# First-stage edge tiles of a graph layer handled in pairs, with the unread matmuls moved

## What is computed

```python
xm = x @ W_n2m;  e = edge_attr @ W_edge
q, k, v = xm @ W_q + b_q, xm @ W_k + b_k, xm @ W_v + b_v
alpha = sum(q[dst] * (k[src] + e @ W_e), per head) / 4
alpha = softmax of alpha over the edges of one dst
out = segment_sum((v[src] + e @ W_e) * alpha, dst)
x_r = xm @ W_skip + b_skip
beta = sigmoid([out, x_r, out - x_r] @ W_beta)
x = layernorm(x + (beta * x_r + (1 - beta) * out) @ W_m2n)
# second layer: x = layernorm(x + relu(x @ w1 + b + segment_sum(ew * (x @ w2)[src], dst)))
```

## Time and profile before

| what | value |
|---|---|
| median of three runs | 1742.92 us |
| span of the profiled execution, first to last instruction | 1705.3 us |
| that execution's time outside the span | not given by the profile |
| busy in the span: PE, DVE, ACT, POOL | 1245.0, 1346.5, 1225.0, 1042.2 us |
| unread matmuls of the first stage (L554) | 784, 118.5 us busy |
| granted TensorE clock, mean of the span | 0.926 of full |

### The profile page before, as it was taken

One profiled execution on the slowest core, in us unless ns is written; L12 is line 12 of the kernel. 1 busy time (PEld: TensorE's weight loads), 2 busy tenths in 40 slices (PEclk: granted clock), 3 DMA queues, 4 the chain that ended last, 5 costly groups with the idle time before them and its releaser, 6 DMA issues.

```text
span 1705.3 us, 34722 instructions
## 1 busy us (share of the span) xinstructions
PE 1245.0 (73%) x9184; PEld 1095.8 (64%) x9184; DVE 1346.5 (79%) x5156; ACT 1225.0 (72%) x4231; POOL 1042.2 (61%) x1182
## 2 busy tenths in 40 slices
PE   1888888888888882288877876788888876665661
PEld 1877777777777772177766766666666675554551
DVE  2777898889999998888877876799999984654653
ACT  0899999999999995077787876899999962222221
POOL 2666666555566660055555656888888846666665
PEclk9999999999999996599999997999999997787876
DMA  6899999999999996734444445899999942222221
GB/s 189 269 306 302 305 305 304 303 302 301 305 301 305 308 300 233 240 117 152 154 144 140 156 141 168 270 289 292 293 289 294 292 143 77 79 82 74 86 77 38
DMA packets 210148, 372.00 MB, mean 218 GB/s; under 512 B 36740, under 2 KB 67821, under 8 KB 208935
## 3 DMA queue, kind: packets, MB, share of 16 engines
q1 hardware_dynamic: 120822, 200.48, 37.2%
q10 hardware_dynamic: 57771, 108.12, 17.3%
q0 software_dynamic: 31360, 61.17, 13.2%
HBM read 231.39 MB, written 161.37 MB: 230 GB/s over the span
## 4 chain that ended last, share of the span: by engine, by line
ACT 36%; DVE 29%; issue 11%; another core or an unknown queue 9%; PE 9%; DMA 1%; POOL 1%; SPq 1%; DVEq 1%; ACTq 0%; POOLq 0%
ACT hout L728 10%; ACT scan_buf L728 10%; DVE stats L992 7%; DVE hpre L1238 6%; ACT big L756 4%; ACT em L688 3%; DVE big L1228 3%; DVE hpre L1314 2%; ACT lv L769 2%; PE pd L596 2%; DVE hout L1002 2%; DVE scan_buf L1002 2%; PE pd L597 2%; PE pk L619 2%
## 5 line engine op out<-in xcount | busy, mean ns | idle before, releaser
L992 DVE BATCH_NORM_STATS2 stats<-hpre 128x6 f32<-128x256 f32 x882 | 334.8, 421 | 1.8
L466 POOL DMA_INDIRECT ring_a<-in_x,gidx x196 | 185.6, 947 | 207.4 <-PE pt L556 146.7
L728 ACT ACTIVATE scan_buf<-hpre,nb,rs 128x128 f32<-128x128 f32 x686 | 292.1, 480 | 2.8 <-DVE scan_buf L1002 1.3
L728 ACT ACTIVATE hout<-hpre,nb,rs 128x128 f32<-128x128 f32 x686 | 292.2, 480 | 2.5 <-issue 1.2
L1098 DVE SCALAR_TENSOR_TENSOR hpre<-pd,beta,xg 128x128 f32<-128x128 f32 x784 | 221.3, 345 | 29.0 <-DVE beta L1091 1.0
L565 PE MATMUL pd<-w_sx,scan_buf 128*128 128x129 f32 x1568 | 229.7, 276 | 0.0
L469 POOL DMA_INDIRECT ring_b<-in_x,gidx x196 | 185.0, 944 | 60.0 <-issue 60.0
L619 PEld LDWEIGHTS pk<-w_sb,scan_buf 128*128 128x128 f32 x1568 | 211.5, 196 | 7.4
L499 POOL DMA_INDIRECT big<-h_tab,gidx x196 | 193.4, 987 | 35.0 <-POOL big L505 29.5
L619 PE MATMUL pk<-w_sb,scan_buf 128*128 128x128 f32 x1568 | 209.9, 278 | 0.0
L565 PEld LDWEIGHTS pd<-w_sx,scan_buf 128*128 128x128 f32 x1568 | 207.0, 192 | 2.7
(11 more groups left out here) (208 smaller groups left out, 3692.4 us busy)
## 6 DMA issues: line engine op xcount, KB each, us to landing
xg<-in_x SPq DMA_DIRECT2D x196, 256.0 KB
scan_buf<-in_xT SPq DMA_DIRECT2D x196, 256.0 KB
val<-h_tab SPq DMA_DIRECT2D x139, 256.0 KB
h_tab<-hout ACTq DMA_DIRECT2D x98, 256.0 KB
h_tab<-scan_buf ACTq DMA_DIRECT2D x98, 256.0 KB
out_z<-hout ACTq DMA_DIRECT2D x98, 256.0 KB
out_z<-scan_buf ACTq DMA_DIRECT2D x98, 256.0 KB
h_two<-h_tab SPq DMA_DIRECT2D x57, 256.0 KB, 9.1
```

The lines of the kernel that those rows point to most:

```text
L466: gp.indirect_dma_start(out=ring_a[:, u, :], out_offset=None, in_=x[:, :], in_offset=bass.IndirectOffsetOnAxis(ap=gidx[:, k, 0:1], axis=0))\
L728: ins = act.activation(hout[ju][:, i * D:(i + 1) * D], hpre[:, ju, i * D:(i + 1) * D], ACT.Identity, bias=nb_of(ju, i), scale=rs_of(ju, i))
L992: ins = dve.bn_stats(stats[:, ju, i, :, :].rearrange("p j s -> p (j s)"), two)
```

## The change

Tiles are worked on in pairs e = k // 2. The transposes of both tiles go to one bank of `pt`, in the order in which they stand in `xT_two`, and one copy of 512 columns moves them in odd steps. The products of both tiles are made in one odd step (k = 2e + 3), one tile in each bank of `pk`; v, q, the multiply and the sum of both follow in the next even step with one instruction each. `v_a`, `q_a`, `pr_a`, `al_a`, `xsT_a` and `kv_a` count pairs. Two unread matmuls (WARM) stand ahead of the products of each tile and write to the unused half of its `pk` bank; the four ahead of the transposes are gone. The softmax pieces start six steps behind instead of two (LAG_S), and four steps with such pieces alone are added at the end.

```diff
--- before.py
+++ after.py
@@ -25,6 +25,8 @@
 LEAD = 60.0
 NZ = 3
 NP = 1
+WARM = 2
+LAG_S = 6
 QSCALE = 1.0 / C ** 0.5
 
 
@@ -332,7 +334,7 @@
                 if j >= 0 and j % 2 == 0:
                     if j == 2 * E1:
                         sp.wait_ge(S["ea_cp2"], 16)
-                    wait(sp, S["kv_a"], j - 2)
+                    wait(sp, S["kv_a"], j // 2 - 1)
                     sp.dma_start(pair[0:R, j // 2 % 2, :], eaT_s[j // 2, :, :]).then_inc(ring["ea_in"][j // 2 % 2], 16)
                 if live(k, 0, T):
                     wait(sp, S["pre_d1"], k - U + 1)
@@ -532,28 +534,29 @@
             pe.wait_ge(S["id1"], 1)
 
             for k in range(T + 2):
-                if k > 1:
-                    j = k - 2
-                    pe.wait_ge(S["xsT_a"], j + 1)
-                    pe.wait_ge(ring["ea_in"][j // 2 % 2], 16 * (j // 4 + 1))
-                    if j > 1:
-                        pe.wait_ge(S["v_a"], j - 1)
-                        pe.wait_ge(S["pr_a"], j - 1)
-                    pe.matmul(pk[:, j % 2, 0:3 * DM], pair[:, j // 2 % 2, j % 2 * P:(j % 2 + 1) * P], b_kvq[:, :],
-                              start=True, stop=False)
-                    pe.matmul(pk[:, j % 2, 0:2 * DM], xT_two[:, j + 2, :], a_kv[:, :], start=False, stop=False)
-                    pe.matmul(pk[:, j % 2, 2 * DM:3 * DM], xT_two[:, j, :], a_q[:, :], start=False, stop=True)\
-                        .then_inc(S["kv_a"], 1)
+                if k > 2 and k % 2 == 1:
+                    e = (k - 3) // 2
+                    pe.wait_ge(S["xsT_a"], e + 1)
+                    pe.wait_ge(ring["ea_in"][e % 2], 16 * (e // 2 + 1))
+                    if e > 0:
+                        pe.wait_ge(S["v_a"], e)
+                        pe.wait_ge(S["pr_a"], e)
+                    for i in range(2):
+                        for w in range(WARM):
+                            pe.matmul(pk[:, i, 2 * P:4 * P], ones3[:, :], bias3[:, 0:2 * P], start=True, stop=True)
+                        pe.matmul(pk[:, i, 0:3 * DM], pair[:, e % 2, i * P:(i + 1) * P], b_kvq[:, :],
+                                  start=True, stop=False)
+                        pe.matmul(pk[:, i, 0:2 * DM], xT_two[:, 2 * e + 2 + i, :], a_kv[:, :], start=False, stop=False)
+                        mm = pe.matmul(pk[:, i, 2 * DM:3 * DM], xT_two[:, 2 * e + i, :], a_q[:, :], start=False, stop=True)
+                    mm.then_inc(S["kv_a"], 1)
                 if k < T:
-                    u = k % U
+                    u, e, i = k % U, k // 2, k % 2
                     pe.wait_ge(ring["xs_in"][u], 16 * (k // U + 1))
                     pe.wait_ge(ring["xd_in"][u], 16 * (k // U + 1))
-                    if k > 1:
-                        pe.wait_ge(S["xsT_a"], k - 1)
-                    for w in range(4):
-                        pe.matmul(pt[:, u % 2, 2 * P:4 * P], ones3[:, :], bias3[:, 0:2 * P], start=True, stop=True)
-                    pe.transpose(pt[:, u % 2, 0:P], ring_b[:, u, :], ident[:, :])
-                    pe.transpose(pt[:, u % 2, P:2 * P], ring_a[:, u, :], ident[:, :]).then_inc(S["t_a"], 1)
+                    if i == 0 and e > 1:
+                        pe.wait_ge(S["xsT_a"], e - 1)
+                    pe.transpose(pt[:, e % 2, i * P:(i + 1) * P], ring_b[:, u, :], ident[:, :])
+                    pe.transpose(pt[:, e % 2, (2 + i) * P:(3 + i) * P], ring_a[:, u, :], ident[:, :]).then_inc(S["t_a"], 1)
 
                     pe.wait_ge(ring["xgT_in"][u], 16 * (k // U + 1))
                     if k > 1:
@@ -739,22 +742,24 @@
 
             def step_a(k, u, it):
                 c = k // TC - 1
-                if 0 <= c < 3 and k % TC == 2 + 5:
+                if 0 <= c < 3 and k % TC == LAG_S + 5:
                     chunk_exps(c)
-                if live(k, 2, T):
-                    j, ju, _ = back(k, u, it, 2)
-                    wait(act, S["kv_a"], j + 1)
-                    wait(act, S["pr_a"], j - 1)
-                    kv = pk[:, ju % 2, DM:2 * DM].rearrange("p (h c) -> p h c", h=H)
-                    vo = val[:, :, :, j] if isinstance(j, int) else \
-                        val[:, :, :, bass.ds(j, 1)].rearrange("p h c a -> p h (c a)")
-                    act.activation(vo, kv, ACT.Copy).then_inc(S["v_a"], 1)
-                    act.activation(q_sb[:, ju % 2, :], pk[:, ju % 2, 2 * DM:3 * DM], ACT.Copy).then_inc(S["q_a"], 1)
+                if k % 2 == 0 and 0 <= k - 4 < T:
+                    e = (k - 4) // 2
+                    act.wait_ge(S["kv_a"], e + 1)
+                    if e > 0:
+                        act.wait_ge(S["pr_a"], e)
+                    kv = pk[:, :, DM:2 * DM].rearrange("p i (h c) -> p h c i", h=H)
+                    act.activation(val[:, :, :, 2 * e:2 * e + 2], kv, ACT.Copy).then_inc(S["v_a"], 1)
+                    act.activation(q_sb[:, :, :], pk[:, :, 2 * DM:3 * DM], ACT.Copy).then_inc(S["q_a"], 1)
+                if k % 2 == 1 and k < T:
+                    e = k // 2
+                    act.wait_ge(S["t_a"], 2 * e + 2)
+                    if e > 0:
+                        act.wait_ge(S["kv_a"], e)
+                    act.activation(xT_two[:, 2 * e:2 * e + 4, :], pt[:, e % 2, :].rearrange("p (a n) -> p a n", a=4),
+                                   ACT.Copy).then_inc(S["xsT_a"], 1)
                 if live(k, 0, T):
-                    wait(act, S["t_a"], k + 1)
-                    wait(act, S["kv_a"], k - 1)
-                    act.activation(xT_two[:, k:k + 3:2, :], pt[:, u % 2, 0:2 * P].rearrange("p (a n) -> p a n", a=2),
-                                   ACT.Copy).then_inc(S["xsT_a"], 1)
                     wait(act, S["mm_d1"], k + 1)
                     wait(act, S["pre_d1"], k - 1)
                     exp_minus(act, em[:, u % 2, :], pd[:, u % 2, :, D], -1.0, S["cl_d1"], S["em_d1"], k)
@@ -1045,11 +1050,11 @@
                                               row[:, a - 1:a] if c else 0.0, ALU.mult, ALU.add)
 
             def scan_piece(k):
-                c, s = (k - 2) // TC - 1, (k - 2) % TC
+                c, s = (k - LAG_S) // TC - 1, (k - LAG_S) % TC
                 if c < 0:
                     return
                 if s < 2:
-                    dve.wait_ge(S["al_a"], (c + 1) * TC)
+                    dve.wait_ge(S["al_a"], -(-(c + 1) * TC // 2))
                     last_piece()
                     local_max(c, 2 * s)
                     piece_done(local_max(c, 2 * s + 1))
@@ -1061,7 +1066,7 @@
                     cut_runs(c).then_inc(S["log_a"], 1)
                 elif 7 <= s < 15:
                     dve.wait_ge(S["sc_act"], c + 1)
-                    dve.wait_ge(S["v_a"], (c + 1) * TC)
+                    dve.wait_ge(S["v_a"], -(-(c + 1) * TC // 2))
                     weigh(c, 2 * (s - 7), 4)
                     piece_done(weigh(c, 2 * (s - 7) + 1, 4))
                 elif s >= 15:
@@ -1070,22 +1075,21 @@
                     piece_done(run_scan(c, 2 * (s - 15) + 1))
 
             def step_a(k, u, it):
-                if live(k, 2, T):
-
-                    j, ju, _ = back(k, u, it, 2)
-                    wait(dve, S["q_a"], j + 1)
-                    dve.scalar_tensor_tensor(out=prod[:, ju % 2, :], in0=pk[:, ju % 2, 0:DM], scalar=QSCALE,
-                                             in1=q_sb[:, ju % 2, :], op0=ALU.mult, op1=ALU.mult).then_inc(S["pr_a"], 1)
+                e = (k - 4) // 2
+                pairs = k % 2 == 0 and 0 <= e < T2
+                if pairs:
+                    dve.wait_ge(S["q_a"], e + 1)
+                    dve.scalar_tensor_tensor(out=prod[:, :, :], in0=pk[:, :, 0:DM], scalar=QSCALE, in1=q_sb[:, :, :],
+                                             op0=ALU.mult, op1=ALU.mult).then_inc(S["pr_a"], 1)
                 scan_piece(k)
                 if live(k, 0, T):
                     wait(dve, S["em_d1"], k + 1)
                     dve.tensor_scalar(ep[:, u % 2, :], em[:, u % 2, :], -1.0, -1.0, ALU.mult, ALU.add)\
                         .then_inc(S["ep_d1"], 1)
-                if live(k, 2, T):
-                    wait(dve, S["pr_a"], j + 1)
-                    ao = alpha[:, :, j:j + 1] if isinstance(j, int) else alpha[:, :, bass.ds(j, 1)]
-                    dve.reduce_sum(ao, prod[:, ju % 2, :].rearrange("p (h c) -> p h c", h=H), AX_X)\
-                        .then_inc(S["al_a"], 1)
+                if pairs:
+                    dve.wait_ge(S["pr_a"], e + 1)
+                    dve.reduce_sum(alpha[:, :, 2 * e:2 * e + 2].rearrange("p h i -> p i h"),
+                                   prod[:, :, :].rearrange("p i (h c) -> p i h c", h=H), AX_X).then_inc(S["al_a"], 1)
                 if live(k, 0, T):
                     wait(dve, S["ep_d1"], k + 1)
                     dve.reciprocal(beta[:, u % 2, :], ep[:, u % 2, :]).then_inc(S["be_d1"], 1)
@@ -1107,11 +1111,11 @@
                 if live(k, 0, T):
                     wait(dve, S["pre_d1"], k + 1)
```

(6 more changed lines are left out.)

## The result

The changed kernel takes 1796.34 us (median of 4 runs, 1790.92 to 1801.44), the kernel before on the same chip 1741.24 us (4 runs, 1738.02 to 1744.43): 1.0322 times as long, 95% interval 1.0287 to 1.0357, 55 us slower. On another chip, where the kernel before took 1704.69 us, the changed kernel took 1767.0 us, 1.0369 (1.0319 to 1.0419), 62 us. Forecast were +69 and 1812.

The account below looks back on a forecast made before the run. ACT was taken to bound the first stage, with a small wait once a pair. Forecast: 1742.9 + 57 (added wait's loop, including 3 for the last tiles) + 12 (PE's clock) = 1812 us, range 1768 to 1885.

Parts of the forecast that it names:

- The loop: First stage: PE's products wait for pair e-1's copy and multiply, delaying later em; 6.81 us a pair against 6.24, +54 us.
- The end of the stage: Last few tiles of the first stage, where ACT had no remote wait and ran 2.91 a tile: some +3 us.
- The clock: PE in the first stage: granted clock sometimes halves after the long wait, 1.3 us per fall; +12 us taken.
- Rival 1: First stage: PE's clock drops in nearly every second pair; 1857 us, 1885 with a wider loop; chance 0.10.
- The time around the span: Outside the profiled span: 37.6 us between 1705.3 and the runs' median 1742.92, left unchanged.
- ACT's copies: First stage, ACT: merged big, val and q_sb copies save 0.18 us a pair, by itself 18 us, at most 47.
- Unread matmuls: PE, first stage: 784 become 392; removal from hpre's wait gives 0, four a pair ahead of products cost 0.43 us.
- ACT bounds the stage before, with a small remote wait once a pair: First stage before the change: ACT 93.8 us busy in 100, waiting some 0.3 us ahead of em once a pair.
- rival 3: First stage: faster, ACT decides; 5.62 a pair and 1684 us without the remote wait, 1725 with it; chance 0.10.
- Rival 2: First stage: PE's signals arrive late; if 0.8 us enters the loop, +76 and 1888 us; chance 0.08.
- The signs named beforehand: Changed profile: PE idle about 2 us a pair, ACT waiting ahead of big and odd em, ACT near 80%, other stages unmoved.
- Two bounds of the range: Whole kernel: low end 1743 + 25 = 1768 (short loop, no drops), high end 1885 (rival 1 in its wide form).

Follow-up runs that it names:

- Two banks: Changed kernel, but both tiles of a pair share one bank of pk and pairs take turns, so products wait for pair e-2: 1694.66 us, 0.9912 of the kernel before.
- rounds of 6.50 and 7.24 us: Changed kernel without unread matmuls in the first stage (6.50): 1770.26 us, ratio 1.0348; with four ahead of each tile's products (7.24): 1842.61 us.
- three gathers: POOL's ring_b gather left out on odd tiles from tile 4: with pairs alternating banks 1691.65 us (0.974, median pair 5.64); on the kernel before 1685.7 us (0.970).

## Why the prediction was right, point by point

- *The loop.* Right in mechanism and in size: 6.81 forecast, 6.81 measured, each link within 0.02; the stage is 56 and 57 us longer in the two pairs of profiles, neither pair certain to be of one chip, where 57 were put in. Two banks, which take away only the added wait, take away all of the loss.
- *The end of the stage*, +3: right in kind, the last pairs run at 6.81 too.
- *The clock*, +12: the term that was mis-sized. The stage of the changed kernel had one stretch at half clock, 6.8 us long and ahead of tile 5, and one of 3.4 us at the same place in the repeated run, worth 1.7 to 3.3 us at 1.65 for 3.4. Those 12 us are most of the difference between 1812 and 1796. The price of a fall was too low (1.3 put in, 1.65 measured), the frequency too high: none in 95 pairs where 12 us stand for nine. A clock row of all 9 was the sign that I had named for a wrong clock term, and it came. The mechanism was real, though: at rounds of 6.50 and 7.24 us, with the same 2.1 us wait, 18 and 24 pairs fell, 30 and some 40 us. The Trainium skill, TensorE: Matmul & The Clock Gate, "A second HAM failure mode", which spoke for such falls, is borne out by those two kernels and not by the changed one. Rival 1 was nearer than its chance looked: a change of 0.3 to 0.4 us in the round would have brought it, though with a fall in every fourth or fifth pair and not in every second.
- *The time around the span*, 37.6: wrong, it is 1.6. It did no harm because the sum was made as a difference.
- *ACT's copies.* 0.18 a pair was the estimate, 0.17 is what showed where ACT was the bound; `val`, `q_sb` and `em` now start 0.17 and 0.16 apart (307.79, 307.96, 308.12). In the changed kernel all of it is off the path, as forecast.
- *Unread matmuls.* 0.43 in the loop for four a pair: exact when added, 0.31 when taken away. In the kernel before, 0 was forecast; removing them gave 0.4% (0.9957, interval just below 1).
- *ACT bounds the stage before, with a small remote wait once a pair.* This was the reading that was incomplete. The remote wait was the bound showing through: the round of POOL's four gathers took 6.2 a pair, and ACT's own work came to 5.8. It did not touch the forecast, since the loop's 6.81 lies above it, but rival 3's "5.62 if the remote wait goes, otherwise 1725" rested on it: 5.64 was measured with three gathers. Two banks, the case in which the loop lets go, came to 0.9912 of before, 1726 on the first chip's scale, and rival 3 with the wait left had 1725.
- *Rival 2, late signals in the loop*: none in the changed kernel, though signals of PE that come late, those of the transposes or of `pd`, are what ACT and POOL wait for in the kernel before and with two banks; the handovers in the changed kernel are those of the earlier trace rows. The slower round leaves the gathers 2.1 us of idle time instead of 1.6.
- *The signs named beforehand* for the loop were there: PE idle about 2 us a pair (put down to `prod` in some places only), ACT's two waits, ACT at 84 of 100 us where I had said near 80. That the other stages should not move can't be told from these profiles to better than the 14 us by which they differ with the chip.
- *Two bounds of the range.* They don't follow from the working: rival 1 in its wide form is 1743 + 89 + 57 = 1889, not 1885, and the short loop was priced at 43, so that without drops it gives 1786; for the 25 behind the 1768 no source is given. The measured time lies inside either way.

## What to carry to other kernels

Before merging two tiles' work, count the banks: if the merged unit needs every bank, the next unit's matmuls wait for its readers, and everything queued behind them joins one loop whose length can be added up from start-to-start times of the profile. A short wait that recurs once a round on the busiest engine, put down to nothing in particular, may be the real bound at work; find the round's other members (here four gathers on an engine that is 60% busy) before pricing a saving on the busy engine. And price a change of PE's waits at neighbouring round lengths too: here the clock fell at 6.50 and 7.24 us and not at 6.81.

## What the runs showed of the hardware that I had not expected

- With one wait of 2.1 us a round on PE, the granted clock fell in 18 of 95 rounds of 6.50 us, in 24 of 95 of 7.24 us, and in none of 95 of 6.81 us, in two executions. A fall cost 1.65 us of a round. Why 6.81 is spared is open.
- With two banks, ACT and POOL resumed 1.2 and 1.4 us after the end of the fourth gather (302.33 and 302.55, behind 301.13), though the transposes for which both wait had ended at 300.63; with three gathers in a round ACT's wait was gone.
- The f32 products of a tile took 0.79 and 0.77 us (304.98, 305.77, 306.54) without unread matmuls ahead of them, 0.72 with.
- 14% fewer bytes at a DMA share of 0.93 moved the time by nothing: a share of 0.93 was no bound here.
- In one execution of the changed kernel a small DMA of the start-up kept DVE waiting 17.3 us (the wait of the kernel after, 0 to 45 us, below), and the gathers started at 39.7 instead of 30.1; in the repeated run the same wait was 3.8 and they started at 29.7. Such a start belongs to the execution, not to the change.

```profile
DVE val L931 <- DMA val<-val: 17.3, 1, 17.3
```
